# The latent attention with other engine lists, and two mixtures that sum and normalise sorted rows and scatter them to DRAM

## The chip, the cores and the metric

One Trainium2 chip, one core of it. The metric is the time on the device in microseconds, median of the runs. One execution was recorded by the hardware profiler.

## The reference

A decoder of four layers in float32 over 32 sequences of 64 tokens and 128 features (2048 rows). Each sublayer is added to its input and the sum is normalised over the 128 features. What matters here is the attention of layer 1, with 16 heads of 64 and keys and values made from a latent of 64 features, and the two mixtures of experts (layer 1 and layer 2):

```python
# layer 1 attention
q = einsum('bsd,qd->bsq', x, wq)                 # 16 heads of 64
kv_latent = einsum('bsd,ld->bsl', x, w_kv_down)  # 64 features
k = einsum('bsl,ql->bsq', kv_latent, w_k_up)
v = einsum('bsl,ql->bsq', kv_latent, w_v_up)
q, k = q*cos + rotate_half(q)*sin, k*cos + rotate_half(k)*sin
probs = softmax(q @ k.T / 8 + causal);  out = (probs @ v) @ wo.T
# layer 1 mixture: one of 8 experts a token, no gate
expert_idx = argmax(xf @ Wr.T + br)
y = relu(xf @ W1[e].T + b1[e]) @ W2[e].T + b2[e]
# layer 2 mixture: at most 80 tokens an expert, gate = probability
gate_prob, pos, keep = ...   # place of a token at its expert, kept if below 80
h = gelu(dispatch @ w1[e] + b1[e]);  out = gate_prob * (h @ w2[e] + b2[e])
```

## The kernel before, in words

The rows lie in SBUF as `state`, 16 tiles of 128 rows (two sequences each). The stages run one after another (`STEPS`, `run_phases`): a narrow attention, a cross attention, a chain of two wide attentions with their GLUs and the latent attention L1_ATTN, a narrow cross attention, the first mixture `moe1`, two narrow attentions, the second mixture `moe2`, two narrow attentions and an FP8 product. Every engine has its own list of work, in program order; semaphores counted per tile (`Turn.wait`) order the engines among each other.

L1_ATTN is one of the chain's parts. `by_tile_steps` runs steps; in a step, each engine does for several tiles what stands in its `step` function, where `tile(k)` is the tile that entered k steps ago. Tiles alternate between two streams, each with its own buffers and four PSUM banks. The depth is 4: a tile is staged, turned, and its queries and keys projected and rotated at `tile(0)`, turned at `tile(1)`, scored and exponentiated at `tile(2)`, mixed and projected at `tile(3)`, normalised at `tile(4)`. The lists are `l1_pool`, `l1_tensor`, `l1_scalar`, `l1_vector`. `rope_wide` makes two products on VectorE, GpSimd adds them (`query_sum`, `key_sum`). `project_keys` uses `latentT` of 64 rows as weights; `mix` multiplies latent keys by the turned probabilities, in 64x64 blocks; `output` applies the product of the value and output weights, made once ahead of the chain. The probabilities are divided by their sums by `normal_probs` on VectorE, ahead of their transposition on TensorE.

The first mixture sorts the tokens by expert into up to 23 tiles of 128 (`SORTED`) with one expert each. VectorE works out the places; GpSimd gathers the rows from a copy of the state in DRAM (`moe_in`) with one indirect DMA for a tile; TensorE turns them and multiplies (`turn`, `up`, `down`), ScalarE applies the ReLU, VectorE fetches each tile's weights (`fetch`) and copies four results at a time out of PSUM (`copy_out`), SP stores them to `moe_out`. When all are stored, GpSimd gathers the 16 tiles back in token order, and for each group of four tiles VectorE adds them to `m_acc` (the state plus the expert's output bias, made by TensorE from the turned one-hot rows) and normalises (`group_norm_pool`, `group_norm_vector`). The second mixture does the same with 8 experts of 80 slots (640 slots in 5 tiles of rows), the bias from `c_bias2`, and the gate `c_best` applied to the gathered rows.

Ahead of a narrow run that follows a mixture, TensorE waits until 12 of the mixture's 16 tiles are done and then runs 16 matmuls on constants (`keep_busy`), and only then waits for the last tile:

```python
if phases[0] in (L2_ATTN, L3_ATTN):
    pe.wait_ge(tile_done, 2 + 16 * phases[0] - 4)
    keep_busy(bank(1, 1) if phases[0] == L2_ATTN else bank(0, 2), 16)
```

## Time and profile before

| what | value |
|---|---|
| median of 3 runs (lowest, highest) | 1622.76 us (1622.22, 1625.02) |
| the profiled execution: time, span | 1620.42 us, 1618.6 us |
| busy share: TensorE, VectorE, GpSimd, ScalarE | 80%, 72%, 51%, 45% |
| L1_ATTN, first staged tile to last sum | about 663 to 906 us |
| first mixture, with routing | about 1010 to 1121 us |
| second mixture, with routing | about 1310 to 1383 us |

Times within a profile are counted from the start of the span. PE is TensorE's matmuls, PEld its weight loads, DVE VectorE, ACT ScalarE, POOL GpSimd. L333 is the line of the helper `mm`, so TensorE's groups are told apart by their operands. In the timeline, instructions of one kind that follow each other are merged into a row with their count; a number in brackets is the idle time of the engine before, with what ended it.

### The profile page before, as it was taken

The numbers are of one execution on the slowest core, as the hardware profiler recorded it, in microseconds if no ns is written. First come the engines' busy times: TensorE is split into PE (matmuls) and PEld (weight loads), VectorE is DVE, ScalarE is ACT, GpSimd is POOL, SyncE is SP. The second block draws the span as 40 slices with busy tenths as digits, with TensorE's granted clock in tenths as the row PEclk, the third lists the DMA queues.
The fourth block names the chain that finished last, engine by engine and source line by source line (L and its number), as shares of the span: only waits on it lengthen the run. The fifth ranks groups of instructions, "written<-read, shape, count | busy, mean of one in ns | idle before, by whom it ended". The sixth has DMA issues, their size and how long they took to land.

```text
span 1618.6 us, 41193 instructions
## 1 busy us (share of the span) xinstructions
PE 1291.4 (80%) x15406; PEld 876.6 (54%) x15406; DVE 1168.8 (72%) x2520; ACT 725.8 (45%) x1486; POOL 824.2 (51%) x1030
## 2 busy tenths in 40 slices
PE   7989869886878868779999788893888883898871
PEld 4556536556645547456666455681555543465540
DVE  6977858984688856568898577434788853798875
ACT  3544435544555544234444354250556521355555
POOL 4543357761377644435453364326557624456654
PEclk9999989997999989879999999795999987899995
DMA  9000000000000000000000000123000012000000
GB/s 340 1 1 1 0 0 0 0 1 22 0 1 0 0 1 14 0 7 1 0 0 1 1 0 3 44 56 132 1 0 1 0 42 35 3 0 2 0 1 26
DMA packets 19559, 29.95 MB, mean 19 GB/s; under 512 B 4291, under 2 KB 16323, under 8 KB 18714
## 3 DMA queue, kind: packets, MB, share of 16 engines
q1 hardware_dynamic: 17562, 24.97, 4.5%
q0 software_dynamic: 1920, 3.94, 1.4%
q8 instruction: 51, 0.84, 0.2%
q14 instruction: 26, 0.21, 0.0%
HBM read 23.91 MB, written 4.98 MB: 18 GB/s over the span
## 4 chain that ended last, share of the span: by engine, by line
PE 41%; DVE 23%; issue 15%; POOL 13%; ACT 6%; DMA 1%; POOLq 1%; DVEq 0%; ACTq 0%; SPq 0%
PE ps L333 32%; DVE maxima L430 6%; PE ps L453 4%; DVE arena L432 4%; PE ps L825 3%; POOL inv_norm L905 3%; ACT arena L440 3%; DVE heads_out L765 2%; POOL arena L910 2%; POOL arena L525 2%; DVE sq_sum L1039 1%; POOL arena L1940 1%; DVE gate L1795 1%; POOL arena L2228 1%; POOL rstd L371 1%
## 5 line engine op out<-in xcount | busy, mean ns | idle before, releaser
L333 PE MATMUL ps<-arena 64*64 64x64 f32 (+5 forms) x7921 | 381.8, 279 | 22.0 <-ACT arena L1222 4.7
L333 PEld LDWEIGHTS ps<-arena 64*64 64x64 f32 (+4 forms) x7921 | 236.2, 134 | 152.7 <-issue 122.3
L525 POOL TENSOR_TENSOR arena<-arena,w_const 128x1024 f32<-128x1024 f32 x96 | 182.3, 1901 | 151.7 <-DVE arena L755 66.7
L430 DVE TENSOR_REDUCE maxima<-ps 128x16 f32<-128x1024 f32 (+1 forms) x144 | 158.5, 1101 | 56.5 <-PE ps L333 52.6
L440 ACT ACTIVATE arena<-arena 128x1024 f32<-128x1024 f32 (+1 forms) x144 | 138.5, 962 | 127.9 <-DVE arena L432 127.0
L453 PE MATMUL ps<-w_const,arena 128*128 128x128 f32 x1024 | 144.1, 283 | 50.8 <-ACT arena L440 34.0
L905 POOL TENSOR_TENSOR inv_norm<-sq_floor,minus_half 128x16 f32<-128x16 f32 x32 | 121.9, 3810 | 86.4 <-DVE sq_floor L1042 86.2
L432 DVE TENSOR_TENSOR arena<-ps,maxima 128x1024 f32<-128x1024 f32 (+1 forms) x144 | 159.3, 1106 | 4.9
L447 ACT COPY arena<-ps 128x1024 f32<-128x1024 f32 (+1 forms) x144 | 131.4, 912 | 56.2 <-PE ps L453 55.7
L453 PEld LDWEIGHTS ps<-w_const,arena 128*128 128x128 f32 x1024 | 116.3, 144 | 74.0 <-ACT arena L440 44.2
L371 POOL TENSOR_TENSOR rstd<-var_eps,minus_half 128x1 f32<-128x1 f32 x144 | 80.5, 570 | 140.7 <-DVE var_eps L873 100.4
L333 PE MATMUL ps<-causal,ident 128*128 128x512 bf16 (+1 forms) x305 | 92.2, 427 | 57.8 <-DVE state L1866 55.0
L765 DVE RECIPROCAL heads_out<-ps 128x128 f32<-128x128 f32 x96 | 91.4, 952 | 53.0 <-PE ps L333 52.7
L333 PE MATMUL ps<-w_fa,shT 128*64 128x256 f32 (+1 forms) x384 | 106.1, 502 | 16.5 <-ACT shT L366 12.1
L689 ACT COPY arena<-ps 64x128 f32<-64x128 f32 x192 | 49.2, 256 | 102.1 <-PE ps L333 100.9
L825 PEld LDWEIGHTS ps<-w_const,arena 128*128 128x128 f32 x512 | 58.6, 144 | 56.8 <-issue 39.5
L825 PE MATMUL ps<-w_const,arena 128*128 128x128 f32 x512 | 70.1, 281 | 23.5 <-POOL arena L910 21.4
L356 PE MATMUL ps<-w_const,xs 128*128 128x128 f32 x192 | 61.2, 321 | 28.4 <-POOL xs L351 27.3
L910 POOL TENSOR_TENSOR arena<-arena 128x1024 f32<-128x1024 f32 x32 | 75.1, 2346 | 7.6 <-DVE arena L856 7.6
L333 PEld LDWEIGHTS ps<-causal,ident 128*128 128x128 bf16 x305 | 30.3, 112 | 88.8 <-DVE state L1866 55.4
L351 POOL COPY xs<-state 128x128 f32 (+1 forms) x144 | 55.1, 384 | 44.5 <-PE ps L333 36.4
L356 PEld LDWEIGHTS ps<-w_const,xs 128*128 128x128 f32 x192 | 27.4, 143 | 84.5 <-issue 45.3
(317 smaller groups left out, 2649.7 us busy)
## 6 DMA issues: line engine op xcount, KB each, us to landing
experts<-in_pack_moe SPq DMA_DIRECT2D x2, 4180.0 KB, 20.3
w_fa<-in_pack_fa SPq DMA_DIRECT2D x2, 1024.0 KB, 11.2
moe_in<-state SPq DMA_DIRECT2D x2, 1024.0 KB, 5.4
w_a<-in_pack_a SPq DMA_DIRECT2D x1, 1824.0 KB, 18.0
moe_out<-arena SPq DMA_DIRECT2D x5, 256.0 KB, 3.5
w_fg<-in_pack_fg SPq DMA_DIRECT2D x2, 537.0 KB, 11.9
ctxT<-in_ctxT SPq DMA_DIRECT2D x1, 1024.0 KB, 7.4
out<-state SPq DMA_DIRECT2D x4, 256.0 KB, 2.3
```

The lines of the kernel that those rows point to most:

```text
L333: return nc.tensor.matmul(o, lhsT, rhs, start=start, stop=stop, skip_group_check=True)
L371: nc.gpsimd.tensor_tensor(rstd[s][:, :], var_eps[s][:, :], minus_half[:, 0:1], ALU.pow)\
L430: nc.vector.reduce_max(mx, sc, X_AXIS).then_inc(signal["max_ready"], 1)
L432: nc.vector.tensor_tensor(probs(s)[:, 0:heads * S].rearrange("p (a h k) -> p a h k", a=2, h=half), sc, mx.unsqueeze(3).broadcast_to([P, 2, ...
L440: nc.scalar.activation(probs(s)[:, 0:n], probs(s)[:, 0:n], ACT.Exp, scale=scale)\
L447: nc.scalar.copy(probsT(s)[:, 0:n], pair(s, 2)[:, 0:n]).then_inc(signal["probsT_ready"], 1)
L453: last = nc.tensor.transpose(pair(s, 2)[:, j * P:(j + 1) * P], probs(s)[:, j * P:(j + 1) * P], ident)
L525: nc.gpsimd.tensor_tensor(keys_wide(s).rearrange("p (b h t) -> p b h t", b=SEQS, h=8), key8(s).rearrange("p (b t) -> p b t", b=SEQS).unsqu ...
L765: nc.vector.reciprocal(heads_out[s][:, :], bank(s, 1, P, 2 * P)).then_inc(signal["sums_inverted"], 1)
L825: last = nc.tensor.transpose(pair(s, first)[:, j * P:(j + 1) * P], source[:, j * P:(j + 1) * P], ident)
L905: nc.gpsimd.tensor_tensor(inv_norm[s][:, :], sq_floor[s][:, :], minus_half[:, :], ALU.pow)\
L910: nc.gpsimd.tensor_tensor(roped(s), roped(s), rope_swapped(s), ALU.add)\
```

## The change

In L1_ATTN the weights for the latent and for the keys are doubled, so that the second half of the key projection works on rows 64 to 127; the mix writes the second sequence's heads with the parities swapped, and the scores place that sequence's heads to match (`swapped`). The order of every engine's list changes: the scores and the softmax's first part come at `tile(1)`, at the end of the step; `normal_probs` moves from VectorE to GpSimd at `tile(3)`; the final normalisation moves from VectorE to ScalarE, with a bias from GpSimd.

In both mixtures the rows stay sorted to the end: residual and output bias (now beside each expert's weights) are added to the sorted rows, statistics, inverse root and normalisation are made on them, and GpSimd scatters each tile into one of two tensors in DRAM that were filled with zeros at the start (rows of unused slots go to a spare tile). At the end both tensors are loaded and added. In the second mixture the gate is carried to the sorted rows in three bf16 parts, each expert has its own gather of 80 rows, and tokens without a slot take the normalised state. The order is that of the lists; some semaphores are merged.

```diff
-        def normal_probs(t, s, heads):
+        def normal_probs(eng, t, s, heads):
@@ l1_pool
                 def step(tile):
                     for t, s in tile(0):
                         stage(t, s)
+                    for t, s in tile(3):
+                        normal_probs(nc.gpsimd, t, s, 16)
+                    for t, s in tile(4):
+                        norm_bias(t, s)
                     for t, s in tile(1):
                         key_sum(t, s)
-                    for t, s in tile(4):
-                        norm_pool(t, s)
                     for t, s in tile(0):
                         query_sum(t, s)
@@ l1_tensor
                 def project_keys(t, s):
                     t.wait("q_parts", s)
                     for k in range(2):
-                        last = mm(bank(s, k), latentT[s], part("a1", "k_up")[0:S, k * 512:(k + 1) * 512])
+                        rows = slice(k * S, (k + 1) * S)
+                        last = mm(bank(s, k), latentT[s][rows, :], part("a1", "k_up")[rows, k * 512:(k + 1) * 512])
...
-                    for b in range(SEQS):
-                        for par in range(2):
+                    for par in range(2):
+                        for b in range(SEQS):
                             rows = slice(par * S, (par + 1) * S)
-                            last = mm(ps[s][rows, 2 + b, :], latent_keys(s)[rows, b, :], probs_of[rows, :, b, :])
+                            turned = slice((par ^ b) * S, ((par ^ b) + 1) * S)
+                            last = mm(ps[s][turned, 2 + b, :], latent_keys(s)[rows, b, :], probs_of[rows, :, b, :])
...
                     for t, s in tile(3):
                         turn_probs_pe(t, 16, streams=(s,), ready="heads_normal")
-                    for t, s in tile(2):
-                        score(t, s)
                     for t, s in tile(0):
                         compress(t, s)
                     for t, s in tile(1):
                         turn_queries(t, s)
                     for t, s in tile(0):
                         project_queries(t, s)
+                    for t, s in tile(3):
+                        mix(t, s)
                     for t, s in tile(1):
                         turn_keys(t, s)
                     for t, s in tile(3):
-                        mix(t, s)
+                        output(t, s)
+                    for t, s in tile(0):
+                        project_keys(t, s)
                     for t, s in tile(1):
                         project_latent(t, s)
-                    for t, s in tile(0):
-                        project_keys(t, s)
-                    for t, s in tile(3):
-                        output(t, s)
+                        score(t, s)
@@ l1_vector
                 def step(tile):
-                    for t, s in tile(2):
-                        softmax_vector(t, 16, streams=(s,))
                     for t, s in tile(0):
                         rotate_queries(t, s)
-                    for t, s in tile(4):
-                        norm_tile(t, s)
                     for t, s in tile(2):
                         row_sums(t, s, 16)
-                        normal_probs(t, s, 16)
                     for t, s in tile(3):
                         add(t, s)
+                        sum_statistics(t, s)
                     for t, s in tile(0):
                         rotate_keys(t, s)
-                    for t, s in tile(3):
-                        sum_statistics(t, s)
+                    for t, s in tile(1):
+                        softmax_vector(t, 16, streams=(s,))
```

On ScalarE the normalisation `norm` stands behind the latent's copy, and the copy of the mixed heads ahead of the exponential. The first mixture's GpSimd and the loads of both:

```diff
+            def return_rows(first, n):
+                for i in range(first, first + n):
+                    pool.wait_ge(ms["m_normed"], i + 1)
+                    if i >= 2:
+                        pool.wait_ge(returned[i % 2], 16 * (i // 2))
+                    nc.gpsimd.indirect_dma_start(moe_back[0][i % 2],
+                                                 bass.IndirectOffsetOnAxis(m_scatter32[:, i:i + 1], 0),
+                                                 out_of(i), None).then_inc(returned[i % 2], 16)
...
+            for j in range(3, SORT_GROUPS):
+                pool.wait_ge(ms["m_up"], 4 * j - 11)
+                if j + 1 == SORT_GROUPS:
+                    set_inverse(pool, 0, *SETS1[0], P)
+                fetch_rows(j)
+            for k, (first, n) in enumerate(SETS1):
+                return_rows(first, n // 2)
+                if k + 1 < len(SETS1):
+                    set_inverse(pool, k + 1, *SETS1[k + 1], P)
+                return_rows(first + n // 2, n - n // 2)
...
+        def load_back(sp, use, order, buffers):
+            for n, k in enumerate(order):
+                sp.wait_ge(returned[k], 16 * (RETURNED1[k] + (EXP // 2) * use))
+                for h in range(2):
+                    sp.dma_start(buffers[k][:, h * 2 * GT:(h + 1) * 2 * GT].rearrange("p (t d) -> p t d", d=D),
+                                 moe_back[use][k][h * 2 * GT:(h + 1) * 2 * GT, :].rearrange("(t p) d -> p t d", p=P))\
+                        .then_inc(back_loaded[2 * n + h], 16)
```

`set_inverse` is an inverse root (`pow`) of one value a tile and a product, on GpSimd. ScalarE's normalisation of tile i stands nine tiles behind its ReLU in the first mixture, four experts behind its GELU in the second. At the end VectorE makes four additions of 128x512, each of which counts four tiles as done. In the second mixture the scatters alternate with `set_inverse` for each two experts, and four groups of products (`c_dropped`) come ahead of the additions. The DMAs that fill the two tensors with zeros:

```diff
+            sp.wait_ge(tables_ready, 1)
+            for m in range(2):
+                for k in range(2):
+                    sp.dma_start(moe_back[m][k][0:TILES * P, :].rearrange("(t p) d -> p t d", p=P),
+                                 shT[0][:, :].unsqueeze(1).broadcast_to([P, TILES, D])).then_inc(blanked, 16)
@@ chain_scalar
+                act.wait_ge(blanked, 4 * 16)
```

## Rows read from the trace of the kernel before

**Rows 1.** Windows: us, busy us (instructions) of PE, PEld, DVE, ACT, POOL; clock; DMA share, GB/s.

```profile
787.30:800.10 12.80, 12.74 (x136) 8.15 (x136) 11.36 (x16) 5.54 (x8) 6.49 (x4) 1.00 0.00 0
...
1010.40:1123.00 112.60, 77.37 (x579) 65.88 (x577) 46.20 (x127) 34.01 (x110) 45.45 (x47) 0.80 0.20 51
```

**Rows 2.** Timeline of TensorE in one step: start, us, what.

```profile
787.45 1.04 PE L453 MATMUL ps<-w_const,arena 128*128 128x128 f32 x8
788.32 0.59 PE L333 MATMUL ps<-causal,ident 128*128 128x512 bf16 x2
788.85 1.16 PE L333 MATMUL ps<-arena 64*64 64x64 f32 x64
789.94 0.43 PE L333 MATMUL ps<-xT,w_a 128*64 128x128 f32 x2
...
793.05 1.04 PE L825 MATMUL ps<-w_const,arena 128*128 128x128 f32 x8
794.02 1.93 PE L333 MATMUL ps<-arena 64*64 64x512 f32 x8
...
796.26 1.98 PE L333 MATMUL ps<-w_a,shT 64*128 64x512 f32 x4
```

**Rows 3.** The same view of VectorE and GpSimd, the step before.

```profile
785.05 1.84 DVE L885 TENSOR_TENSOR arena<-arena,inv_sum 128x1024 f32<-128x1024 f32 x1
...
783.43 2.38 POOL L1090 TENSOR_TENSOR arena<-arena 128x1024 f32<-128x1024 f32 x1 [2.97 <-DVE arena L856]
...
785.76 1.28 POOL L351 COPY xs<-state 128x128 f32 x1
```

**Rows 4.** Windows: one rotation of the queries on VectorE.

```profile
780.94:783.26 2.32, 2.28 (x14) 0.68 (x14) 2.32 (x4) 2.06 (x3) 0.00 (x0) 1.00 0.00 0
```

**Rows 5.** Groups: line, instruction, count | busy, mean ns | idle before, releaser.

```profile
L525 POOL TENSOR_TENSOR arena<-arena,w_const 128x1024 f32<-128x1024 f32 x96 | 182.3, 1901 | 151.7 <-DVE arena L755 66.7
...
L440 ACT ACTIVATE arena<-arena 128x1024 f32<-128x1024 f32 (+1 forms) x144 | 138.5, 962 | 127.9 <-DVE arena L432 127.0
...
L905 POOL TENSOR_TENSOR inv_norm<-sq_floor,minus_half 128x16 f32<-128x16 f32 x32 | 121.9, 3810 | 86.4 <-DVE sq_floor L1042 86.2
```

**Rows 6.** Timeline: start of the last full step, last sum of L1_ATTN.

```profile
863.88 1.04 PE L453 MATMUL ps<-w_const,arena 128*128 128x128 f32 x8
...
905.62 0.29 DVE L1264 TENSOR_TENSOR total<-state,ps 128x128 f32<-128x128 f32 x1 [5.06 <-PE ps L333]
```

**Rows 7.** Timeline of the first mixture, from the first sorted rows on.

```profile
1037.43 1.09 PE L2006 MATMUL ps<-w_const,arena 128*128 128x128 f32 x4 [3.02 <-DMA arena<-moe_in,arena]
...
1088.11 0.56 DVE L2163 COPY arena<-ps 128x384 f32<-128x384 f32 x1 [3.68 <-PE ps L333]
...
1101.20 1.05 POOL L1849 TENSOR_TENSOR arena<-arena,minus_half 128x4 f32<-128x4 f32 x1
...
1116.31 5.32 PE L333 MATMUL ps<-causal,ident 128*128 128x512 bf16 x16 [26.77 <-DVE state L1866]
...
1121.46 0.39 PE L356 MATMUL ps<-w_const,xs 128*128 128x128 f32 x2
```

**Rows 8.** Timeline of the second mixture: gathers, last expert, warm-up, next stage.

```profile
1328.62 1.06 POOL L2221 DMA_INDIRECT arena<-moe_in,arena  x1 [19.24 <-DVE arena L2404]
...
1329.99 0.94 POOL L2221 DMA_INDIRECT arena<-moe_in,arena  x1 [0.31 <-issue]
...
1332.01 0.27 PE L2274 MATMUL ps<-w_const,arena 128*128 128x128 f32 x1
...
1347.88 0.69 DVE L2418 TENSOR_TENSOR arena<-ps,arena 80x512 f32<-80x512 f32 x1 [5.73 <-PE ps L333]
...
1376.91 6.41 PE L333 MATMUL ps<-causal,ident 128*128 128x512 bf16 x16 [28.21 <-DVE state L1866]
...
1383.69 0.47 PE L356 MATMUL ps<-w_const,xs 128*128 128x128 f32 x2 [0.37 <-POOL xs L351]
```

**Rows 9.** DMA issues: size, median us to landing.

```profile
moe_in<-state SPq DMA_DIRECT2D x2, 1024.0 KB, 5.4
```

573 lines of the change are left out of this document (318 added, 255 removed).

## The prediction

> **What bounds the kernel now.** I read the windows by stage first, then the timeline of one step of the third wide attention (the latent one, L1_ATTN) engine by engine, then the two mixtures in order of time, and last the groups that price what the change moves. The profiled execution has a span of 1618.6 us and a time of 1620.4 us; the median of the runs shown is 1622.8 us, 2.3 us above it.
>
> In a full step of L1_ATTN (one tile) TensorE is busy for 12.74 of 12.80 us at a granted clock of 1.00, VectorE for 11.36, GpSimd for 6.49, ScalarE for 5.54 [rows 1]. TensorE sets the pace. Six steps lie between 787.45 and 863.88, so a step takes 12.74 us [rows 2, 6]; it takes as long in the 11 steps after the ramp.
>
> The mixtures are chains: in the window of the first, TensorE is busy for 77 of 113 us at a mean clock of 0.80 [rows 1]. In both, nearly half the stage is one thing after another: store the sorted results, gather them back, normalise group by group. In the first, TensorE ends its experts at 1088, the last copy out starts at 1088.11 and the next attention's first transpose at 1121.46 [rows 7]: 33 us with TensorE idle but for a clock warm-up. In the second it is 1347.88 to 1383.69, 36 us [rows 8].
>
> **L1_ATTN, what leaves TensorE.** Keys: two matmuls of 64 rows x 512 columns both from rows 0 to 63, four instructions in a row, 1.98 us [rows 2]. The duplicated weights put the second on rows 64 to 127. Mix: 8 instructions of 64x64 and 512 columns, 1.93 us [rows 2], now in two quadrants at a time; the new target partitions and order use all four. The scores show what four quadrants give: 64 instructions in 1.16 us [rows 2], 18 ns each, where a 64-column instruction alone, by the mix's 0.48 us for a pair of 512 columns, would need some 60 ns. So four quadrants do run together, two row groups over the same columns among them. I take half for both: 0.95 + 0.95 us off, 12.74 - 1.9 = 10.8 us of TensorE work a step. If neither overlaps, nothing comes off.
>
> The mix lets both row groups write one PSUM bank at once, in different partitions. The old mix does so already, and its 8 instructions need the time of 4 [rows 2]. The Trainium skill (TensorEngine Tiling (Array Packing), Gotcha 1: PSUM Pressure) says that different row tiles cannot access the same bank simultaneously; by it the new mix would stay at 1.9 us, and the old one would have been slower than it is. The trace speaks against it.
>
> **L1_ATTN, what moves.** Normalising the probabilities goes from VectorE to GpSimd. On VectorE it takes 1.84 us, and the two collide: it starts at 785.05 under a GpSimd addition that ends at 785.81, and the 128x128 copy that GpSimd starts at 785.76 takes 1.28 us [rows 3], ending 0.15 us after VectorE's operation. That collision goes. On GpSimd the price is between 1.90 us (128x1024 with both inputs spread) and 2.38 us (128x1024, two full inputs) [rows 5, 3]; the new operation has one input spread and one full, so 2.1 us. The final normalisation goes to ScalarE (some 0.5 us, hidden by its idle 7 us), with a bias operation of 0.3 us on GpSimd. VectorE falls to some 9.5 us a step, GpSimd rises to 8.5, ScalarE to 6.
>
> What is late next is a loop through three engines, because normalising now stands on GpSimd behind the query sum, and TensorE's transposes of the probabilities come early in its list. From the start of those transposes: 0.87 us of them (787.45 to 788.32), then latent, query transposes and query projection (789.94 to 793.05, 3.1 us, 0.2 of it a wait that goes) [rows 2], so 3.8 us; rotation on VectorE 2.4 us [rows 4]; query sum 2.38 us and copy 0.29 us on GpSimd; normalising 1.9 to 2.4 us; and 0.2 us of handing over. Sum 11.0 to 11.5 us, against 10.8 us of TensorE work. I take a step of 11.2 us: 1.5 us x 11 steps = 17 us.
>
> Ends of the stage: the scores move one step earlier, so the last tile needs one drained step less before its softmax. Today the way from the start of step 15 to the last sum is 863.88 to 905.62, 41.7 us [rows 6]. The same walk by the new lists (11.2 for the step, some 9 to the last scores, then one after another the operations of 128x1024 on VectorE and ScalarE at 1.0 to 1.2 us each [rows 5], normalising 2.1, transposes, mix 0.9, output 2) gives 34 to 36 us: 7 us off. The ramp in is worth 2 us (two shorter key projections at half clock), the new order puts 2.4 us of softmax ahead of the last GLU tile there, so -1 to +4. L1_ATTN together: 17 + 7 + 2 = 26, less 0.5 for the bias on the way out: **-25 us, between -16 and -31**.
>
> **First mixture.** Gathers start as before; the first rows are transposed at 1037.43, as they land [rows 7]. The removed one-hot transposes and bias matmuls lay in TensorE's wait for them: nothing gained, some 0.5 us of warmth lost. The experts stay bound by TensorE (16 instructions and a share of transposes, about 1.93 us a tile), and end near 1088 again. ScalarE gets a normalisation for each tile and comes close to that pace: 0 to 2 us of delay.
>
> Removed behind 1088: store, 16 gathers at 1.25 us, four group norms. Added: 23 scatters to DRAM from GpSimd, each waiting until the one two before it has landed, and four loads of 512 KB. An indirect DMA costs 0.94 + 0.31 us on GpSimd [rows 8]. The landing of a scatter is in no row. Nearest: a first gather issued at 1328.62 is used at 1332.01, 3.4 us [rows 8]; 1 MB moves in 5.4 us [rows 9], and 64 KB is a sixteenth of it. I take 2.7, a little under the first gather, with 2 and 4 as bounds. Scatter 0 can start once the last gathers are out, at 1064; with one inverse root of 4 columns (1.05 us [rows 7] and a product of 0.3) for every four tiles, and the roots queued between scatters, four tiles take 6.7 us, near the pace of the experts. The last three sets wait for each other (statistics, root, norm, scatter): scatter 14 at 1090, the root of set 5 at 1096, scatter 22 at 1103, landed at 1106. The loads: 1 MB takes 5.4 us from issue to landing [rows 9]; the second follows by 3 us, so the last lands at 1112.5, four additions of 0.69 us with it: state whole at 1114 against 1120.8.
>
> Then a cost that the change doesn't touch by name. TensorE starts 16 warm-up matmuls when 12 of the 16 tiles are done. Today groups of four end 6 us apart, so the 5.32 us of warm-up (1116.31) are just over when the last tile is staged (1121.46) [rows 7]. Now groups three and four end 0.7 us apart, and the warm-up holds TensorE until 1113.5 + 5.4 to 6.4 = 1119.5. **-2 us, between -6 and +8** (12 us for each us of landing above 3).
>
> **Second mixture.** The statistics of all 16 tiles (some 6 us of small operations, an estimate) fall into VectorE's wait for the logits, the root of 16 columns (3.81 us [rows 5]) and 16 norms lie under the routing. The gate in three bf16 parts adds some 2 us of small operations ahead of the counts; behind them the quotient, the remainder and a third of the one-hot rows go, some 3 us: first gather 1 us earlier. Eight gathers instead of five feed experts of 1.9 us; VectorE's new work for each pair, near TensorE's pace, and ScalarE waiting for a root behind a scatter cost some 2 us: last expert at 1349 against 1347.9. Then roots and scatters: 4 and 5 at 1353 and 1355, 7 at 1358, landed 1361; loads until 1368; additions until 1370; warm-up of 6.41 us [rows 8] from 1369.3 to 1375.7 against 1383.7. **-8 us, between -12 and +2.**
>
> **The rest.** 4 MB of zeros written to DRAM at the start stand on SP's queue behind all weights and are awaited only by ScalarE before the wide attentions, near 230 us: nothing. 0.5 MB more of weights for each mixture lands under other stages.
>
> Sum: 1618.6 - 25 - 2 - 8 = 1583.6; with 1.8 outside the span and 2.3 to the median, **1588 us**.
>
> **The rivals.** (1) The quadrants don't overlap further (row groups write one bank, or the key tiles run in turn). For: no row shows 64x128 tiles in pairs. Against: the scores' 18 ns. TensorE stays at 12.5 us a step, 3 us instead of 17: 1602 us. The skill's rule above is the part of this for the mix alone, worth 0.9 us a step beyond the loop's 11.2: 1593 us. (2) GpSimd is slower than its rows (normalising over 2.4, or descriptor work held up by VectorE): a step of 12.2 us, and each mixture 3 us later: 1605 us. (3) Slower than before: the landing of a scatter. GpSimd waits in order for scatter i-2, so from about 3.5 us on the first mixture holds 12 landings in a row and the second 4. From the starts above (scatters from 1064 and 1343, then loads, additions, warm-up) the two give 16 L - 67 us for a landing of L us; L1_ATTN's 25 us are used up at L = 5.7. At 6.5 us a scatter: 1635 us. Against it, the gather of this size took 3.4 us [rows 8]. The Trainium skill (DMA: Bandwidth & Descriptors, Anatomy of one DMA) gives 2.0 us plus 0.15 us for 64 KB and says that the delay can be surprisingly long when the target is HBM; by the figure the pace of the roots decides, by the warning this rival does. (4) The change doesn't do what it says: the results are put together in another way but all parts are exercised in every run, so it has no chance of its own.
>
> **How the numbers follow.** Forecast 0.72; rival 1 0.12 (the mix alone 0.05 of it); rival 2 0.10; rival 3 0.06. The forecast's own parts give 1576 to 1600. Leaving out 2 in 10: **1574 to 1606**. A measurement here tells 0.2% (3 us) from no change. Only rival 3 and the worst of rival 2 end above 1619: faster 0.93, same 0.02, slower 0.05.
>
> **What would show it.** Steps of 11.0 to 11.5 us in L1_ATTN with TensorE waiting 0.2 to 0.7 us for GpSimd's normalising before the transposes; the key and mix groups at about 1.0 us; the 1.28 us copy at 0.29. In the mixtures, indirect DMAs 1.3 to 1.4 us apart with gaps for the roots; the additions close together; warm-up matmuls ending 4 to 5 us after the last addition. The forecast is wrong if a step stays above 12 us, if the gaps between scatters are above 2 us, or if the experts of the first mixture end later than 1091 on the old clock.

## The result

Measured beside the kernel before, the changed kernel takes 1612.89 us (median of 6 runs, 1610.28 to 1617.19) against 1622.49 us (6 runs): ratio 0.9938, 95% interval 0.9917 to 0.9959. It is faster, by 10 us where 34.5 were forecast, and outside the forecast range. The same kernel was measured in four more sets, each beside the kernel before on one chip:

| run | after, us | before, us | ratio (95%) | fourth fetch | experts end | next attention starts |
|---|---|---|---|---|---|---|
| result | 1612.9 | 1622.5 | 0.9938 (0.9917 to 0.9959) | 43.2 | 93.2 | 125.3 |
| after_again | 1610.2 | 1625.6 | 0.9916 (0.9894 to 0.9939) | 41.5 | 90.9 | 124.4 |
| after_third | 1599.5 | 1624.4 | 0.9855 (0.9824 to 0.9887) | 35.4 | 81.7 | 114.5 |
| after_fourth | 1601.8 | 1622.5 | 0.9877 (0.9848 to 0.9906) | 35.4 | 82.0 | 114.7 |
| after_fifth | 1607.7 | 1626.1 | 0.9892 (0.9847 to 0.9937) | 38.9 | 91.3 | 125.2 |
| before (first profile) | | | | 35.1 | 77.7 | 111.1 |
| attn_only (old mixture, see Experiments) | | | | 34.5 | 75.0 | 108.7 |

The last three columns are of the first mixture in the profiled run, in us after its store of the state (1010.37 in before, 996.11 in after): VectorE's fourth fetch of expert weights, the end of the last expert product, and the first transpose of the next attention. One program has two levels there, some 10 us apart, and what follows keeps them apart. The profile of before belongs to the upper one by its missing landing events (448 of the 624 of the first mixture's gathers are recorded, all 624 in attn_only), so the old mixture at the lower level is the row of attn_only. The four later sets ran on four different chips, and the chip of the first is not on record.

### The profile page after: what moved, and what is told of

Same layout as the page of the kernel before. It is cut to its first block, busy times and chain, and to the rows that moved or that the text cites. A ratio compares the mean times of both kernels' runs of the same rounds, so it can differ in the third digit from the quotient of the medians.

```text
span 1610.7 us, 41365 instructions
## 1 busy us (share of the span) xinstructions
PE 1274.3 (79%) x15361; PEld 875.4 (54%) x15361; DVE 1142.0 (71%) x2545; ACT 749.8 (47%) x1545; POOL 855.7 (53%) x1078
## 4 chain that ended last, share of the span: by engine, by line
PE 39%; DVE 23%; issue 14%; POOL 12%; ACT 7%; DMA 2%; another core or an unknown queue 1%; POOLq 1%; DVEq 1%; SPq 0%; ACTq 0%
PE ps L339 31%; DVE maxima L436 6%; PE ps L459 4%; DVE arena L438 4%; DVE heads_out L769 3%; ACT arena L446 2%; POOL arena L914 2%; POOL inv_norm L909 2%; POOL arena L531 2%; PE ps L829 2%; DVE sq_sum L1043 1%; ACT arena L1235 1%; DMA moe_back<-arena 1%; DVE gate L1811 1%
## 5 line engine op out<-in xcount | busy, mean ns | idle before, releaser
L339 PE MATMUL ps<-arena 64*64 64x64 f32 (+5 forms) x7921 | 374.6, 279 | 30.9 <-DVE arena L2191 9.0
L453 ACT COPY arena<-ps 128x1024 f32<-128x1024 f32 (+1 forms) x144 | 131.2, 911 | 40.8 <-PE ps L459 40.3
L339 PE MATMUL ps<-causal,ident 128*128 128x512 bf16 (+1 forms) x305 | 87.2, 408 | 46.0 <-DVE state L2234 25.9
L914 POOL TENSOR_TENSOR arena<-arena 128x1024 f32<-128x1024 f32 x32 | 75.1, 2348 | 7.5 <-DVE arena L861 7.5
L357 POOL COPY xs<-state 128x128 f32 (+1 forms) x144 | 43.5, 304 | 66.0 <-PE ps L339 37.9
L1094 POOL TENSOR_TENSOR arena<-arena 128x1024 f32<-128x1024 f32 x16 | 37.8, 2359 | 66.2 <-DVE arena L861 66.2
```

The costliest lines, as they stand in the source:

```text
L339: return nc.tensor.matmul(o, lhsT, rhs, start=start, stop=stop, skip_group_check=True)
L453: nc.scalar.copy(probsT(s)[:, 0:n], pair(s, 2)[:, 0:n]).then_inc(signal["probsT_ready"], 1)
L914: nc.gpsimd.tensor_tensor(roped(s), roped(s), rope_swapped(s), ALU.add)\
```

## The profile after

Windows of the changed kernel (us; busy us and instructions of PE, PEld, DVE, ACT, POOL; granted clock; DMA share; GB/s): a full step of the third wide attention, its end, and the first mixture.

```profile
771.43:782.66 11.23, 11.11 (x133) 7.39 (x134) 9.35 (x15) 5.89 (x9) 7.40 (x7) 1.00 0.00 0
859.20:889.70 30.50, 22.71 (x265) 15.62 (x261) 12.72 (x25) 11.80 (x15) 10.72 (x11) 0.85 0.01 1
996.10:1121.40 125.30, 75.05 (x522) 63.97 (x521) 46.40 (x154) 40.67 (x127) 57.30 (x62) 0.77 0.22 59
```

The step is 11.23 us where it was 12.80 in the window of [rows 1], TensorE still busy for all of it, VectorE down to 9.35, GpSimd up to 7.40. TensorE's own work in that step, against [rows 2]:

```profile
771.60 1.04 PE L459 MATMUL ps<-w_const,arena 128*128 128x128 f32 x8
...
775.38 1.09 PE L339 MATMUL ps<-arena 64*64 64x512 f32 x8
...
779.59 1.13 PE L339 MATMUL ps<-w_a,shT 64*128 64x512 f32 x4
...
781.57 1.16 PE L339 MATMUL ps<-arena 64*64 64x64 f32 x64
782.66 0.33 PE L362 MATMUL ps<-w_const,xs 128*128 128x128 f32 x1
```

The mix is the row at 775.38, 1.09 us for the 1.93 of before; the keys are at 779.59, 1.13 us for 1.98. So the four quadrants run together. Over the loop the steps average 11.32 us (850.65 - 726.09 over 11, the turns of tiles 4 and 15). GpSimd's part of a step:

```profile
766.55 2.36 POOL L1094 TENSOR_TENSOR arena<-arena 128x1024 f32<-128x1024 f32 x1 [3.13 <-DVE arena L861]
768.84 0.30 POOL L357 COPY xs<-state 128x128 f32 x1
769.09 1.92 POOL L890 TENSOR_TENSOR arena<-arena,inv_sum 128x1024 f32<-128x1024 f32 x1
```

The query sum, the 128x128 copy and the normalising stand one behind the other; the copy takes 0.30 us (1.28 in [rows 3]), the normalising 1.92. It is done at 771.01. TensorE turns the next tile at 771.43 and starts the transposes that read its result at 771.60; between tile 4 and tile 15 no wait of TensorE for GpSimd stands in the trace. So the forecast wait of 0.2 to 0.7 us is absent, and the 11.2 us of TensorE's own work (122.9 of 124.7 us busy over the 11 steps) set the pace.

The start of the experts of the first mixture, TensorE, ScalarE and VectorE (start, us, engine, line, operation, tiles, idle time before and what ended it):

```profile
1024.68 3.78 PE L339 MATMUL ps<-arena 128*128 128x128 f32 x16 [0.68 <-issue]
...
1026.79 1.14 ACT L2087 ACTIVATE arena<-ps,arena 128x128 f32<-128x128 f32 x4 [2.16 <-issue]
...
1029.89 2.33 PE L339 MATMUL ps<-arena 128*128 128x128 f32 x16
...
1032.08 1.14 ACT L2087 ACTIVATE arena<-ps,arena 128x128 f32<-128x128 f32 x4 [4.15 <-remote]
1033.28 1.16 PE L339 MATMUL ps<-arena 128*128 128x128 f32 x8 [1.06 <-issue]
...
1034.93 0.59 ACT L2075 COPY arena<-ps 128x512 f32<-128x512 f32 x1 [1.71 <-remote]
...
1039.30 1.14 ACT L2087 ACTIVATE arena<-ps,arena 128x128 f32<-128x128 f32 x4 [3.78 <-remote]
1039.32 0.70 DVE L2191 COPY arena<-experts 128x1028 f32 x1 [13.79 <-remote]
```

TensorE's group at 1024.68 holds the up-projections of tiles 0 and 1 and ends at 1028.46, but ScalarE's relu of tile 1 starts at 1032.08. The group at 1029.89 holds the down-projection of tile 0, which frees the buffer of the fourth fetch, and the up-projection of tile 2; it ends at 1032.2, and both who wait for it start at 1039.3. "remote" is the profile's word for a signal whose sender it doesn't find. In after_third, the same code:

```profile
1021.73 3.79 PE L339 MATMUL ps<-arena 128*128 128x128 f32 x16 [0.67 <-ACT arena L2075]
...
1023.85 1.14 ACT L2087 ACTIVATE arena<-ps,arena 128x128 f32<-128x128 f32 x4 [2.17 <-PE ps L339]
1025.56 1.14 ACT L2087 ACTIVATE arena<-ps,arena 128x128 f32<-128x128 f32 x4 [0.56 <-PE ps L339]
...
1026.96 7.68 PE L339 MATMUL ps<-arena 128*128 128x128 f32 x64
...
1028.53 0.74 DVE L2191 COPY arena<-experts 128x1028 f32 x1 [5.95 <-PE ps L339]
```

Every signal arrives in time, and TensorE runs through. Behind the experts both levels look alike; the changed kernel again:

```profile
1102.76 0.97 POOL L1967 DMA_INDIRECT moe_back<-arena  x1 [0.76 <-DMA moe_back<-arena]
1104.04 0.97 POOL L1967 DMA_INDIRECT moe_back<-arena  x1 [0.30 <-issue]
1105.76 0.97 POOL L1967 DMA_INDIRECT moe_back<-arena  x1 [0.75 <-DMA moe_back<-arena]
1106.30 3.95 SPq L1903 DMA_DIRECT2D arena<-moe_back  x4
1114.13 1.29 DVE L2234 TENSOR_TENSOR state<-arena 128x512 f32<-128x512 f32 x2 [21.71 <-DMA arena<-moe_back]
1115.85 1.29 DVE L2234 TENSOR_TENSOR state<-arena 128x512 f32<-128x512 f32 x2 [0.43 <-DMA arena<-moe_back]
1116.60 5.01 PE L339 MATMUL ps<-causal,ident 128*128 128x512 bf16 x16 [25.86 <-DVE state L2234]
...
1117.30 0.53 POOL L357 COPY xs<-state 128x128 f32<-128x128 f32 x2 [10.56 <-DVE state L2234]
...
1121.45 0.38 PE L362 MATMUL ps<-w_const,xs 128*128 128x128 f32 x2
```

Scatters go in pairs 3.0 us apart, each pair released by the landing of the one before. The additions are whole at 1117.1, the last tile of the first pair is staged at 1117.8, and the warm-up holds TensorE until 1121.4.

## Experiments

The sets compare kernels on one chip; sets 2 and 5 (after_again, after_fifth) are at the upper level, sets 1, 3 and 4 at the lower. In a single profile the length of a stage says more than the time at which it ends: tile 2 of the third wide attention is turned anywhere from 690.6 to 699.9 us in runs whose code is the same up to there. Lengths wander less: from the last turned tile to the next attention it is 42.5 us in after and 41.9 in after_fifth.

**attn_only** (set 1). The attention's edits in the kernel before; the mixtures are the old ones.

```
-   "k_up": rows_to(i["L1_attn_w_k_up"].T, P),
+   "k_up": np.concatenate([i["L1_attn_w_k_up"].T] * 2, axis=0),
... (and the attention's lists of the diff)
```

> The kernel before with the change of the third wide attention alone: duplicated down and k_up weights, the two row groups for keys and mix, normalising and the bias on GpSimd, the final normalisation on ScalarE, the new order on all engines. Both mixtures are as before. Theory A (the changed kernel got all its gain from this attention and gave part of it back in the first mixture): the attention ends 16 us earlier as in the changed kernel, its last sum near 889.7 against 905.6, a step of 11.3 us, and the whole kernel is 15 to 16 us faster than before, near 1607, which is faster than the full change (1612.9). The first mixture then takes its old length: from the complete state to the first matmul of the next attention 111 us, as 1010.4 to 1121.5 before. Rival B (the mixture is slow for what stands before it, for instance the code of the attention, and not for its own change): the first mixture takes 124 us here too, as in the changed kernel, and the whole is within 3 us of the kernel before.

Measured: 1609.8 us, ratio 0.9939 (0.9919 to 0.9960); steps of 11.33 us, 42.8 us from the last turned tile to the next attention's first transpose (42.5 in after, 44.8 in before), first mixture 108.7 us to that point. Rival B falls: the old mixture keeps its length behind the new attention, and is 2.4 us shorter than in before. Theory A holds in its parts, but the whole gained 10 us and not 15: tile 2 began 5 us later than in before, within the wandering said above. It is no faster than the full change at the same level (ratios 0.9855 and 0.9877), since at that level the second mixture gains more (64.2 for 72.1 us) than the first loses (114.5 for 108.7). Of attn_only's first mixture, whose store is at 999.73, the last expert product and the next attention's first transpose:

```profile
1073.57 1.16 PE L333 MATMUL ps<-arena 128*128 128x128 f32 x8 [0.34 <-ACT arena L2073]
...
1108.43 0.38 PE L356 MATMUL ps<-w_const,xs 128*128 128x128 f32 x2
```

**hold_gathers, base_later, early_warmup** (set 1).

```
 # hold_gathers (GpSimd)
-fetch_rows(2)
-for j in range(3, SORT_GROUPS):
-    pool.wait_ge(ms["m_up"], 4 * j - 11)
+for j in range(2, SORT_GROUPS):
+    pool.wait_ge(ms["m_up"], {2: 1, 3: 4, 4: 6, 5: 9}[j])
 # base_later (VectorE)
 fetch(i)
-base(i)
+base(i - 2)
 # early_warmup (TensorE)
-pe.wait_ge(tile_done, 2 + 16 * phases[0] - 4)
+pe.wait_ge(back_loaded[1], 16 if phases[0] == L2_ATTN else 32)
```

> The changed kernel, with the gathers of the first mixture held in smaller lots: groups 2 to 5 wait for 1, 4, 6 and 9 finished up-projections (groups 3 to 5 waited for 1, 5 and 9, and group 2 for none), so that 12 gathers follow each other instead of 16. Theory C (while GpSimd issues gathers one behind the other, ScalarE and VectorE see TensorE's signals late: relu of tile 1 starts 3.6 us after the matmul it waits for, fetch 3 starts 8 us after, and both are released 2.5 us after the last of the 16 gathers): the fourth expert fetch starts some 5 us earlier after the complete state than the 43.2 us of the changed kernel, near 38, and the experts end 3 to 5 us earlier; the kernel is 2 to 5 us faster than the changed one, near 1609. Rival D (the stall is instruction loading or another thing that does not follow the gathers): the fourth fetch stays at 43 us after the complete state or moves for no reason that the gathers give, and the time stays at 1613.

> The changed kernel, with VectorE's sum of a sorted row tile and the output bias (base) moved two fetches back in its list: base(i-2) behind fetch(i). So the wait for the scatter 12 tiles ago no longer stands ahead of the next two fetches. Theory E (this wait delays the fetches: VectorE stood 2.7, 4.1, 2.3 and 3.1 us before base and TensorE 1.7, 0.8 and 0.8 us for VectorE's fetch): TensorE's waits for the fetch go, the experts end 3 to 4 us earlier, near 1085.5 instead of 1089; since the scatters behind the experts follow at 3.0 us a pair and were late already, the kernel gains 1 to 3 us, near 1611. Rival F (the scatters set the end alone): the experts end earlier but the last scatter keeps its time, 1105.8, and the kernel stays at 1613. The stall at the start of the experts (fetch 3 at 43.2 us after the complete state) must stay in this run by theory C of the gathers, with 16 gathers in a row; if it goes, the register reads and base waits ahead of fetches 1 to 3 made it.

> The changed kernel; TensorE's 16 warm-up matmuls ahead of the second and third narrow pairs start when the second of the four loads of the returned rows has landed, not when 12 of the 16 tiles are added. In the changed kernel the warm-up ran 1116.6 to 1121.6 while the last tile was staged at 1117.8, and 1369.1 to 1373.8 with the tile staged at 1370.4. Theory G (the warm-up itself is on the path): it now runs 1112 to 1117, the first transpose follows the staged tile, and each of the two places gains 3 to 3.7 us: 6 to 7 us in all, near 1606. Rival H (the matmuls behind it wait for something else, such as ScalarE's bias copy or the weights): the first transpose moves by less than 1 us in each place and the time stays above 1611.

Measured: 1601.0 us (ratio 0.9878, 0.9847 to 0.9909), 1596.5 us (0.9859, 0.9823 to 0.9894) and 1594.9 us (0.9857, 0.9821 to 0.9893). All three went 9 to 15 us below what the changed kernel's ratio of 0.9938 gives here, more than any theory gave, and the fourth fetch came after 33.4, 34.0 and 35.4 us: the delay was gone in all of them, base_later and early_warmup with the same 16 gathers in a row included. So this set could not test theory C, and these ratios are to be held against after_third and after_fourth, from which they can't be told. The stages do tell. In base_later the experts end 75.3 us after the store (81.3 and 81.8 in the two runs beside it, 81.7 in after_third), the next attention starts at 109.3 (114.0 in hold_gathers, 114.5 in after_third). That is where the old mixture's experts end, 75.0 in attn_only of the same set. The waits that went are these, of after_third's VectorE:

```profile
1049.10 0.29 DVE L2200 TENSOR_TENSOR arena<-arena,experts 128x128 f32<-128x128 f32 x1 [2.69 <-DMA moe_back<-arena]
...
1055.64 0.29 DVE L2200 TENSOR_TENSOR arena<-arena,experts 128x128 f32<-128x128 f32 x1 [3.56 <-DMA moe_back<-arena]
...
1064.26 0.29 DVE L2200 TENSOR_TENSOR arena<-arena,experts 128x128 f32<-128x128 f32 x1 [2.33 <-DMA moe_back<-arena]
...
1073.69 0.29 DVE L2200 TENSOR_TENSOR arena<-arena,experts 128x128 f32<-128x128 f32 x1 [3.14 <-DMA moe_back<-arena]
```

Each is a sum into a buffer whose scatter, 12 tiles ago, has not landed (the first scatter is issued 53.0 us after the store, behind the last gather), and the next fetch stands behind it; from the fourth fetch to the end of the experts base_later takes 41.3 us for 46.3. The fourth fetch itself comes at 34.0 for 35.4, but it wanders from 33.4 to 35.5 in the sets without the delay. In all some 6 us of expert time (6.4 against after_third, 6.0 and 6.5 against the runs beside it), more than the 3 to 4 of theory E; 5.2 of them reach the next attention, so rival F falls. In early_warmup (TensorE, the additions, the staging, first mixture):

```profile
1105.53 6.01 PE L339 MATMUL ps<-causal,ident 128*128 128x512 bf16 x16 [21.65 <-DMA arena<-moe_back]
1107.40 1.29 DVE L2234 TENSOR_TENSOR state<-arena 128x512 f32<-128x512 f32 x2 [21.71 <-DMA arena<-moe_back]
1109.14 1.29 DVE L2234 TENSOR_TENSOR state<-arena 128x512 f32<-128x512 f32 x2 [0.45 <-DMA arena<-moe_back]
...
1110.58 0.53 POOL L357 COPY xs<-state 128x128 f32<-128x128 f32 x2 [10.61 <-DVE state L2234]
1111.38 0.38 PE L362 MATMUL ps<-w_const,xs 128*128 128x128 f32 x2
```

The first transpose follows the staged tile. From the end of the experts to it: 29.0 us instead of 32.8, and 19.8 instead of 23.9 in the second mixture. Theory G holds, 3.8 and 4.1 us. The second mixture's experts also end 2.9 us earlier in that run (37.4 for 40.3), which this edit doesn't explain.

**after_again, exp_first, tail_busy, combo** (set 2).

```
 # exp_first (ScalarE)
+exp_scalar(t, 16, 0.125, streams=(s,))
 heads_mixed(t, s)
-exp_scalar(t, 16, 0.125, streams=(s,))
 # tail_busy (TensorE, for the last tile)
+keep_busy(bank(0, 2), 10)
 turn_probs_pe(t, 16, streams=(s,), ready="heads_normal")
+keep_busy(bank(0, 2), 4)
 mix(t, s)
+keep_busy(bank(0, 2), 4)
 output(t, s)
```

> The changed kernel once more, not a line of it altered. In its first profile TensorE's signals reached ScalarE and VectorE up to 8 us late at the start of the experts of the first mixture (fourth fetch 43.2 us after the state was complete). In three kernels that differ from it by a few instructions the fourth fetch came after 33.4, 34.0 and 35.4 us, in one of them with the same 16 gathers in a row. Theory I (the stall belongs to that measurement and not to the program): the fourth fetch comes after 34 to 36 us here too, the experts end some 81 us after the complete state instead of 93, and the kernel runs in about 1602, ratio near 0.989. Theory J (the stall belongs to exactly this program, for instance to where its instructions lie): the fourth fetch comes after 43 us again, and the time is 1611 to 1613, ratio 0.994.

> The changed kernel with ScalarE's exponential of a tile (step lag 2) ahead of its copy of the mixed heads (lag 3) in the third wide attention, as the order was before. Theory K (the end of this attention was mis-sized because the exponential stands behind the copy of the mixed heads, which waits for TensorE): in the changed kernel the exponential of the last two tiles started 1.0 and 2.1 us after VectorE's difference; both go to under 0.2, and the last sum comes 2 us earlier after the last turned tile, 37 us instead of 39.0. Steps stay at 11.3 us. The kernel gains 2 us against the changed one. Rival L (the end is set by GpSimd's normalising behind the query sum, and TensorE at half clock): the last sum stays at 39 us and the time does not move.

> The changed kernel with warm-up matmuls on TensorE in its idle time at the end of the third wide attention: 10 ahead of the last transposes of probabilities, 4 ahead of the last mix and 4 ahead of the last output product, into a bank that nothing uses. In the changed kernel these three groups took 1.55, 1.98 and 3.78 us for the last tile where they take 1.09, 1.09 and 2.05 in a full step, at a mean granted clock of 0.85 over the end of the stage. Theory M (the end was mis-sized by TensorE's clock): the three groups go back to 1.1, 1.1 and 2.1 us, and the last sum comes 3 us earlier, 36 us after the last turned tile instead of 39.0; the kernel gains 2 to 3 us. Rival N (the added matmuls are longer than the idle time, or the clock falls all the same): no gain, or up to 2 us of loss.

> The changed kernel with four edits at once: base two fetches later, warm-up matmuls of the narrow pairs started by the second load, ScalarE's exponential ahead of the copy of mixed heads, and the warm-up matmuls at the end of the third wide attention. If the parts add (base later 6 us of expert time, of which some 5 reach the next stage; early warm-up 3.5 us twice; exponential 2; clock at the end 3): 17 us faster than the changed kernel without its stall (about 1602), so near 1585. If the last two do not work as thought, 1590.

Measured: after_again 1610.2 us with the delay (fourth fetch 41.5), so theory I falls; theory J was not right either, as after_third showed. exp_first 1608.0 us (ratio 0.9902, 0.9875 to 0.9930), tail_busy 1608.4 us (0.9901, 0.9876 to 0.9927): each 2 us under after_again, within the error, so the stage decides. From the last turned tile to the next attention's first transpose it is 42.5 us in after_again, 41.2 in exp_first, 39.6 in tail_busy. Theory M holds with 2.9. Theory K was right at most in direction: 1.3 us instead of 2, and only 0.7 against the 41.9 that the unaltered attention takes in after_fifth and base_later, whose first tiles are spaced as in exp_first. With both edits (combo, combo3) it is 39.1: 3.4 us in all under after_again, not the sum of the two. The last tile's transposes, mix and output, first in the changed kernel, then in tail_busy:

```profile
880.02 1.55 PE L459 MATMUL ps<-w_const,arena 128*128 128x128 f32 x8 [2.43 <-POOL arena L890]
...
882.76 1.98 PE L339 MATMUL ps<-arena 64*64 64x512 f32 x8 [1.19 <-ACT arena L453]
...
885.87 3.78 PE L339 MATMUL ps<-arena 128*128 128x128 f32 x16 [1.12 <-ACT arena L1235]
```

```profile
876.17 2.32 PE L339 MATMUL ps<-causal,ident 128*128 128x512 bf16 x10
...
878.76 1.09 PE L459 MATMUL ps<-w_const,arena 128*128 128x128 f32 x8 [0.27 <-POOL arena L890]
879.69 1.03 PE L339 MATMUL ps<-causal,ident 128*128 128x512 bf16 x4
...
881.22 1.09 PE L339 MATMUL ps<-arena 64*64 64x512 f32 x8 [0.50 <-ACT arena L453]
...
883.43 2.05 PE L339 MATMUL ps<-arena 128*128 128x128 f32 x16 [0.15 <-ACT arena L1242]
```

In the changed kernel the granted clock of 880.0 to 889.6 is 0.53 of full speed, that is mostly its lower level of 1.2 GHz, and the three groups take 7.3 us; with TensorE kept busy they take 4.2, at 1.00 from 876.1 to 885.5 (2.4 GHz). combo took 1596.5 us (0.9817, 0.9792 to 0.9843), 13.7 under after_again with the delay still in it (fourth fetch 38.9); its expectation was 17 us from a kernel without the delay, near 1585.

**after_third, hold_relu, scat_free, combo3** (set 3).

```
 # hold_relu (GpSimd)
-fetch_rows(2)
-for j in range(3, SORT_GROUPS):
-    pool.wait_ge(ms["m_up"], 4 * j - 11)
+for j in range(2, SORT_GROUPS):
+    pool.wait_ge(ms["m_relu"], {2: 2, 3: 4, 4: 7, 5: 9}[j])
 # scat_free (GpSimd)
-if i >= 2:
-    pool.wait_ge(returned[i % 2], 16 * (i // 2))
+if i >= 4:
+    pool.wait_ge(returned1[i % 4], 16 * (i // 4))
```

> The changed kernel, unaltered, as the measure for the three runs beside it. In two of the sets so far TensorE's signals came late at the start of the experts of the first mixture (fourth fetch 38.9 to 43.2 us after the complete state) and VectorE's first bias sum of the second mixture stood 5.3 to 5.8 us for a signal of unknown source; in the set with hold_gathers, base_later and early_warmup neither did. So every kernel of a set shows the delay or none does. Theory: this run and the three beside it agree again, whichever way. Time 1610 to 1613 with the delay, 1602 without.

> The changed kernel with at most 8 gathers in a row in the first mixture: groups 2, 3, 4 and 5 wait for ScalarE's relu of 2, 4, 7 and 9 tiles. Theory C again (the late signals come from GpSimd's unbroken row of gathers, in those sets that show them at all; the second mixture, whose 8 gathers are unaltered, tells whether this set does): with the delay in the second mixture, the fourth fetch here comes at 34 to 36 us where the unaltered kernel beside it has 41 to 43, and the experts end 6 to 9 us earlier; the kernel is some 8 us faster than after_third. Rival O (the delay is tied to the place and not to the number of gathers in a row): the fourth fetch stays at 39 us or later. If this set shows no delay, the two kernels are within 2 us.

> The changed kernel with the first mixture's scatters waiting for the scatter four before, not two before; each scatter has rows of its own for the padding, so two in flight to one tensor write different rows. Theory P (the landing of a scatter sets the pace behind the experts: pairs 3.0 us apart, 1.5 us a scatter, where two indirect DMAs and nothing else take 1.27 us each): the last scatter comes 3 to 4 us earlier after the last expert than the 17 us of the changed kernel, with GpSimd's waits for moe_back at zero, and the kernel gains 3 us against after_third. VectorE's wait before base for the scatter 12 tiles ago stays about as it is. Rival Q (roots, norms and the experts set the pace): the last scatter moves by under 1 us and the time stays.

> The changed kernel with all edits: base two fetches later, scatters waiting for the fourth before, gathers in lots behind relu in the first mixture and behind gelu in the second, warm-up of the narrow pairs started by the second load, the exponential ahead of the mixed heads and warm-up matmuls at the end of the third wide attention. The four edits of combo gave 14 us against the changed kernel in their set. If the lots remove the late signals (8 us in the first mixture, 2 in the second) and the freed scatters give 3: 25 us faster than after_third in a set with the delay, near 1585, and 17 us without, near 1585 as well. If theory C is wrong: 1592 in a set with the delay.

Measured: after_third 1599.5 us, the unaltered kernel, 11 and 13 us below its other two medians: the set decides. hold_relu 1605.5 us (0.9892, 0.9861 to 0.9922), 6 us above after_third where at most 2 had been expected: without the delay the lots cost, since the last gather, and with it the first scatter, come 3 us later (56.0 for 53.0 us after the store) and VectorE's waits before base rise from 11.7 to 15.5 us. scat_free 1603.2 us (0.9864, 0.9831 to 0.9896): GpSimd's waits for landings fall from 4.7 to 0.3 us and the last scatter comes 14.8 us after the experts instead of 16.6, the last scatters are 1.3 us apart, a landing takes 2.3 us at the median and 4.4 at most, but the next attention starts at 114.4 as before (32.0 us behind the experts for 32.8). Rival Q holds in the main. combo3 1582.3 us (0.9741, 0.9715 to 0.9768) is the fastest, 17 us under after_third as expected and 42 us under before: experts end at 78.0, next attention starts at 105.6, in the second mixture at 60.4 (64.2).

**after_fourth, lots, after_fifth, lots_again** (sets 4 and 5). lots is hold_relu with the second mixture's gathers 5 to 8 each behind one gelu.

> The changed kernel, unaltered, as the measure for the run beside it: with the delay its fourth fetch comes 41 to 43 us after the complete state and the first bias sum of the second mixture stands 5.3 to 5.8 us; without it 35.4 us and none. Time 1610 to 1613, or 1600.

> The changed kernel with the gathers in lots in both mixtures: in the first at most 8 in a row, then 4 at a time behind ScalarE's relu of 2, 4, 7 and 9 tiles; in the second 4 in a row, then one behind each gelu. If the unaltered kernel beside it shows the delay: theory C (the end of the row of gathers releases the signals) has the fourth fetch at 34 to 36 us and no long wait of unknown source in either mixture; rival O (the place) has the fourth fetch at 39 us or later and the second mixture's 5 us wait too. If the unaltered kernel shows no delay, this run tells nothing about it, and takes 1605 like hold_relu.

> The changed kernel, unaltered, beside lots_again. In the sets with the delay so far the trace also lacked landing events of the gathers (14 to 31 of 64 for four gathers of the third and fourth lot, against 64 of 64 in the sets without). If this set shows the delay, the fourth fetch comes 41 to 43 us after the complete state, landing events are missing, and the time is 1610 to 1613; if not, 35.4 us, all landing events, and 1600.

> As for lots. If the unaltered kernel beside it shows the delay: theory C (the end of the unbroken row of gathers releases the signals) has the fourth fetch at 34 to 36 us and no wait of unknown source above 2 us in either mixture; rival O (the place) has the fourth fetch at 39 us or later and the second mixture's 5 us wait too. Without the delay beside it, 1604 as before, and nothing is told.

Set 4 had no delay (after_fourth 1601.8, lots 1604.5 us) and tells nothing of it. Set 5 had it. Waits of the second mixture, first after_fifth, then lots_again (engine, line, waited for: us, times, longest):

```profile
DVE arena L2493 <- remote: 5.0, 1, 5.0
```

```profile
ACT arena L2387 <- PE ps L339: 12.5, 6, 7.3
...
DVE arena L2494 <- PE ps L339: 8.2, 5, 3.2
```

With gathers in lots the wait of unknown source is gone there, and in the first mixture the fourth fetch comes after 34.6 us beside 38.9. For the two places it was asked of, the delay follows the row of gathers, as theory C has it, on one profile of each kernel. It is not cured, and theory C's limit of 2 us for any such wait is broken: the second and the third lot together are again 8 gathers in a row, and behind them relu and fetches wait up to 2.5 us for a signal of unknown source, for instance:

```profile
1034.14 1.14 ACT L2086 ACTIVATE arena<-ps,arena 128x128 f32<-128x128 f32 x4 [1.86 <-remote]
...
1035.72 0.85 DVE L2190 COPY arena<-experts 128x1028 f32 x1 [2.08 <-remote]
```

The experts end at 89.1 us (91.3), and the time is the same, 1607.6 and 1607.7 us. In the second mixture the wait costs nothing: its last expert product ends 40.3 us after the store in after_third and in after_fifth.

## Why the prediction was wrong

The profiled run, span against forecast: 1610.7 - 1583.6 = 27.1 us. 9.7 of it are the third wide attention, 16.2 the first mixture, -0.8 the second, 2.0 the stages between and behind, which the change doesn't touch.

**The step: right in size, not in what bounds it.** 11.32 us for 11.2, 15.5 us gained for 17. The forecast gave TensorE 10.8 us of work and let a loop through VectorE and GpSimd's normalising set 11.2; the trace has 11.2 us of TensorE's work, some 0.3 of it since mix and keys came to 1.09 and 1.13 us and not to half of 1.93 and 1.98, and no wait for the normalising. So the step agrees in part by luck. That two row groups write one PSUM bank at once without cost stands: 8 instructions in 1.09 us. The statement of the Trainium skill (TensorEngine Tiling (Array Packing), Gotcha 1: PSUM Pressure) does not hold for this mix. Rivals 1 and 2 fall (normalising took 1.90 to 1.94 us, an indirect DMA 0.97 us and 0.30 between two). The price of rival 1 for the mix alone was 0.9 us a step beyond the loop's 11.2; its own terms give 10.8 + 0.95 - 11.2, some 0.55.

**The ends of the attention: mis-sized.** I walked the last tile through the new lists with each operation at its duration in a full step and got 7 us of gain; it was 2.2. Of the 4.8 us that lack, tail_busy gives back 2.9: TensorE's lower clock, since the last tile now waits for VectorE, ScalarE and GpSimd with nothing else for TensorE to do. ScalarE's exponential behind the mixed heads is 0.5 to 1.3 us; both together are 3.4, and 1.4 stay open. The ramp in, forecast at -2, was +2.4 from tile 4 of before to tile 4 of after, inside the wandering of that place; no run was made for it.

**The first mixture, experts: the step that failed.** The forecast let them stay bound by TensorE and end near 1088 on the old clock, 77.7 us after the store, with 0 to 2 us for ScalarE. It has no term for the sums of residual and bias on VectorE, nor for what is queued behind their waits. The sum waits for the scatter 12 tiles ago, and the next fetch stands behind it. Without the delay the experts end 81.7 us after the store where the old mixture's, at the same level, end at 75.0; moving the sums two fetches back gives 75.3. So the missing term is some 6 us. Against the 77.7 of before, whose profile is at the upper level, only 4 of it show. A short operation that nobody needs soon has its wait ahead of the copies that feed the slowest engine.

**The delay: not foreseen.** In the upper sets another 9 to 12 us are lost between the first gathers and the end of the experts; in the profiled run it is the larger part of the 16.2 us. The old kernel had 12 gathers in a row, and its upper profile is 2.7 us longer than attn_only's to the end of the experts; the new one has 16. That its TensorE has few signals in reserve, and so loses more, is argued and not shown.

**Behind the experts: right in sum, wrong in the cadence.** 32.2 to 33.9 us against the forecast's 31.5. The landing was sized well (2.7 taken; 2.3 at the median in scat_free, 4.4 at most), and rival 3 falls. The figure of the Trainium skill (DMA: Bandwidth & Descriptors, Anatomy of one DMA), some 2.15 us for 64 KB, is near the 2.3; its warning of a long delay to HBM is not borne out here. But a pair takes 3.0 us, not twice 1.3 to 1.4, since each pair waits for the landing of the last; in scat_free, without that wait, the last scatters are 1.3 us apart. The warm-up held TensorE as forecast.

**Second mixture: right, by two errors that cancel.** From the store to the next attention's first transpose 64.7 us for 73.5, 8.8 gained for 8. The experts end 2.8 us later than in before, where 1.1 were forecast, and the way behind them takes 24.3 us for 26.7.

The sign named in advance fired: "if the experts of the first mixture end later than 1091 on the old clock". They ended at 1103.6, and at 1092 in the sets without the delay. In those sets the kernel took 1599.5 and 1601.8 us, 12 and 14 above the forecast and inside its range of 1574 to 1606; the delay took it out.

## What to carry to other kernels

Before costing an added operation at nothing, write down what its wait is queued ahead of: here a 0.29 us sum held up the weight fetches of the whole chain, for some 6 us. A stage's end runs on the same durations as its middle only if TensorE stays busy, so price the tail at the lower clock or fill the gap. And measure a kernel in more than one set before explaining ten microseconds of it. Here the same program had two levels, and stages are to be compared at one level only: held against the one early profile of before, the missing term looked like 4 us, and at one level it is some 6.

## What was not expected of the hardware

- In some sets TensorE's signals reached ScalarE and VectorE up to 8 us late while GpSimd issued a long row of indirect gathers, from some 12 us after the first of them; in after the last of them came 2.6 us behind the row's end. It costs the changed kernel some 10 us. In the old mixture before is 2.4 us longer than attn_only, on one profile of each.
- The same traces also lack landing events: of the 64 of gathers 5 to 8, 19, 20 and 23 are recorded in result, after_again and after_fifth, all 64 in after_third and after_fourth. The profile of before lacks such events too. Whether one congested path causes both, whether the recording itself takes part, and whether the chip makes a set of the one or the other kind, no run settles: no chip was used for two of the later sets.
- A group of 16 warm-up matmuls (128x512, bf16) took 5.0 to 6.4 us, begun from idle, and held up the next stage: starting them by the landing of the second load gave 3.8 and 4.1 us in the two places.
